# One wait per piece of weights instead of four in the down projection of a transformer block

## The reference

```python
x = x + attn(layernorm(x), wq, wk, wv, wo)
xn = layernorm(x)
g = einsum('th,ih->ti', xn, gate_w) * gate_s      # 2048 -> 5632
u = einsum('th,ih->ti', xn, up_w) * up_s
hdn = silu(g) * u
x = x + einsum('ti,hi->th', hdn, down_w) * down_s  # 5632 -> 2048
```

## Time and profile before

| | |
|---|---|
| median of 3 runs | 3502.85 us |
| the profiled execution, its own time | 3511.11 us |
| its slowest core (core 3), first to last instruction | 3509.5 us |
| spans of the 8 cores | 3486.0 to 3509.5 us |
| PE matmul busy on core 3 | 2981.4 us (85%), 13472 matmuls |
| VectorE, ScalarE busy | 930.2 us (27%), 896.3 us (26%) |
| mean granted TensorE clock, cores | 0.909 to 0.922 of 2.4 GHz |
| down projection, first span | about 1893 to 2348 us |
| down projection, second span | about 3030 to 3489 us |

### The profile page before, as it was taken

One profiled execution on the slowest core, in us unless ns is written; L12 is line 12 of the kernel. 1 busy time (PEld: TensorE's weight loads), 2 busy tenths in 40 slices (PEclk: granted clock), 3 DMA queues, 4 the chain that ended last, 5 costly groups with the idle time before them and its releaser, 6 DMA issues.

```text
span 3509.5 us, 43939 instructions; the slowest of 8 cores (3486.0 to 3509.5 us)
## 1 busy us (share of the span) xinstructions
PE 2981.4 (85%) x13472; PEld 1390.3 (40%) x13472; DVE 930.2 (27%) x1998; ACT 896.3 (26%) x1744; POOL 83.1 (2%) x158
## 2 busy tenths in 40 slices
PE   4999977777779969999998787677999999868766
PEld 2454444444434444444443232224444444323222
DVE  4532178888823121111110102112111111010111
ACT  2420056666622032222221121103222222101000
POOL 0000000000000000000000000000000000000000
PEclk9999976777689969999999899896999999989888
DMA  6212210000062234444444334323444444333432
GB/s 157 97 35 39 37 34 6 8 8 8 3 136 87 91 87 117 108 120 114 108 122 96 86 106 114 84 58 99 109 113 121 109 116 119 98 85 100 113 85 59
DMA packets 69058, 297.67 MB, mean 85 GB/s; under 512 B 7780, under 2 KB 14052, under 8 KB 49380
## 3 DMA queue, kind: packets, MB, share of 16 engines
q1 hardware_dynamic: 44360, 204.67, 17.7%
q0 software_dynamic: 24480, 90.19, 15.1%
HBM read 364.03 MB, written 20.97 MB: 110 GB/s over the span
## 4 chain that ended last, share of the span: by engine, by line
PE 78%; issue 8%; DVE 6%; DMA 6%; ACT 2%; DVEq 0%; ACTq 0%; SPq 0%; POOLq 0%
PE pb L849 18%; PE pb L745 17%; PE pb L751 17%; PE pb L445 6%; PE pb L682 6%; PE pb L518 4%; DMA out<-osb 3%; DVE pb L487 2%; PE pb L404 2%; PE pb L653 2%; PE pb L473 1%; PE pb L386 1%; ACT xnst L643 1%; PE pb L522 1%; DMA wot<-wot 1%
## 5 line engine op out<-in xcount | busy, mean ns | idle before, releaser
L745 PE MATMUL pb<-xn2T,gub 128*128 128x512 bf16 x2816 | 639.1, 380 | 0.0
L751 PE MATMUL pb<-xn2T,gub 128*128 128x512 bf16 x2816 | 636.5, 379 | 0.0
L849 PE MATMUL pb<-dnb,h_a 128*128 128x512 bf16 x2240 | 543.4, 386 | 101.4 <-PE pb L849 88.1
L745 PEld LDWEIGHTS pb<-xn2T,gub 128*128 128x128 bf16 x2816 | 276.0, 98 | 334.1 <-issue 3.9
L751 PEld LDWEIGHTS pb<-xn2T,gub 128*128 128x128 bf16 x2816 | 275.6, 98 | 332.2
L849 PEld LDWEIGHTS pb<-dnb,h_a 128*128 128x128 bf16 x2240 | 201.9, 98 | 443.0 <-issue 251.0
L756 ACT ACTIVATE silub<-pb,gs_sb 128x512 f32<-128x512 f32 x176 | 121.2, 689 | 929.2 <-PE pb L745 929.2
L770 DVE SCALAR_TENSOR_TENSOR h_a<-pb,us_sb,silub 128x512 bf16<-128x512 f32 x144 | 108.1, 751 | 889.1 <-PE pb L751 889.1
L518 PE MATMUL pb<-idf,pr 128*128 128x128 f32 x768 | 201.6, 393 | 90.8 <-DVE stats L504 87.1
L809 ACT CAST dnb<-dnf 128x2048 bf16<-128x2048 f32 x44 | 83.6, 1899 | 764.2 <-PE pb L849 672.1
L682 PE MATMUL pb<-wot,aoall 128*128 128x512 bf16 x1024 | 228.8, 387 | 18.9 <-DMA wot<-wot 18.9
(11 more groups left out here) (77 smaller groups left out, 1919.2 us busy)
## 6 DMA issues: line engine op xcount, KB each, us to landing
gf<-gt SPq DMA_DIRECT2D x88, 1024.0 KB, 5.7
gub<-ut POOLq DMA_DIRECT2D x88, 512.0 KB, 7.2
dnf<-dnt SPq DMA_DIRECT2D x44, 1024.0 KB, 4.9
dnb<-dnt POOLq DMA_DIRECT2D x44, 512.0 KB, 5.2
xb<-xo SPq DMA_DIRECT2D x16, 1024.0 KB, 4.8
xb<-xo SPq DMA_DIRECT2D x32, 512.0 KB, 5.0
out<-osb SPq DMA_DIRECT2D x64, 256.0 KB, 2.8
wqb<-wqt POOLq DMA_DIRECT2D x16, 512.0 KB, 5.2
```

Source lines behind the costliest of these rows:

```text
L745: e.matmul(ph(gb), lhsT=gub[gsl][:, dc, :], rhs=xn2T[:, dc, 512 * grp:512 * grp + 512], start=(dc == 0), stop=(dc == DC - 1))
L751: e.matmul(ph(ub), lhsT=gub[usl][:, dc, :], rhs=xn2T[:, dc, 512 * grp:512 * grp + 512], start=(dc == 0), stop=(dc == DC - 1))
L849: e.matmul(ph(tt), lhsT=h_ap(i, tt), rhs=dnb[dsl][:, k, :], start=(i == 0), stop=(i == IC - 1))
```

## The change

The four operations of a piece become one. For `i4` > 0, one operation of 32 matmuls replaces four of 8. For `i4` = 0, the eight single matmuls stay, and one operation of 24 (k = 1 to 3) replaces three of 8. The matmuls, their operands and their order are the same. The first operation of 24 or 32 names what the replaced ones named together: the inner blocks `r_h`, the piece's weights, the eight banks.

```diff
-            for k in range(4):
-                i = 4 * i4 + k
-                if i == 0:
-                    for tt in range(8):
-                        em("tensor", ... e.matmul(ph(tt), lhsT=h_ap(0, tt), ...
-                    continue
-                em("tensor", lambda e, i=i, k=k, dsl=dsl: [
-                    e.matmul(ph(tt), lhsT=h_ap(i, tt),
+            if i4 == 0:
+                for tt in range(8):
+                    em("tensor", ... e.matmul(ph(tt), lhsT=h_ap(0, tt), ...
+                em("tensor", lambda e, dsl=dsl: [
+                    e.matmul(ph(tt), lhsT=h_ap(k, tt),
                              rhs=dnb[dsl][:, k, :],
-                             start=(i == 0), stop=(i == IC - 1))
-                    for tt in range(8)],
-                   reads=[r_h[i], r_dnb[dsl]],
-                   writes=[r_pb[tt] for tt in range(8)], n=8)
+                             start=False, stop=False)
+                    for k in range(1, 4) for tt in range(8)],
+                   reads=[r_h[1], r_h[2], r_h[3], r_dnb[dsl]],
+                   writes=[r_pb[tt] for tt in range(8)], n=24)
+            else:
+                em("tensor", lambda e, i4=i4, dsl=dsl: [
+                    e.matmul(ph(tt), lhsT=h_ap(4 * i4 + k, tt),
+                             rhs=dnb[dsl][:, k, :],
+                             start=False, stop=(4 * i4 + k == IC - 1))
+                    for k in range(4) for tt in range(8)],
+                   reads=[r_h[4 * i4 + k] for k in range(4)] + [r_dnb[dsl]],
+                   writes=[r_pb[tt] for tt in range(8)], n=32)
```

More of the change, by code:

```diff
@@ L836, in build_nc @@
                 ln2_stats(1, (ci - 4) // 4)
-            for k in range(4):
-                i = 4 * i4 + k
-                if i == 0:
-                    for tt in range(8):
[L841 to L846, removed]
-                    continue
-                em("tensor", lambda e, i=i, k=k, dsl=dsl: [
-                    e.matmul(ph(tt), lhsT=h_ap(i, tt),
-                             rhs=dnb[dsl][:, k, :],
-                             start=(i == 0), stop=(i == IC - 1))
-                    for tt in range(8)],
-                   reads=[r_h[i], r_dnb[dsl]],
-                   writes=[r_pb[tt] for tt in range(8)], n=8)
+            if i4 == 0:
+                for tt in range(8):
+                    em("tensor", lambda e, tt=tt, dsl=dsl:
+                       e.matmul(ph(tt), lhsT=h_ap(0, tt),
+                                rhs=dnb[dsl][:, 0, :],
+                                start=True, stop=False),
+                       reads=[r_h[0], r_dnb[dsl]],
+                       writes=[r_pb[tt]])
+                em("tensor", lambda e, dsl=dsl: [
+                    e.matmul(ph(tt), lhsT=h_ap(k, tt),
+                             rhs=dnb[dsl][:, k, :],
+                             start=False, stop=False)
[10 more added lines that the diff above has]
+                   writes=[r_pb[tt] for tt in range(8)], n=32)
             if ci + 2 < NCH:
```

## The result

The changed kernel takes 3385.07 us in the median of 10 runs (3379.55 to 3723.24). The ratio to the kernel before is 0.965, with a 95% interval of 0.9637 to 0.9662: 3.5% faster. The forecast was 3378 us and 124.5 us off 3502.85, a ratio of 0.9645. The five runs that are left of before have a median of 3507.2 us, the seven of after 3384.16, which is 123.0 us apart. The profiled execution of after took 3381.15 us, 130.0 less than that of before, and is read on its slowest core, core 6.

A forecast was written before the change was run, and what follows sets the result against it. The prediction took TensorE, waiting for its own last matmul in the down projection, as the bound: 256 x 0.494 = 126.5 us, less 2.0 absorbed, gives 124.5 off 3502.85, or 3378.4 us, range 3364 to 3400.

The forecast's parts named there:

- 256 waits of PE for the matmul just issued: Down projection groups: merging removes 256 of 344 waits of PE for its own last matmul, 0.494 us each, 126.5 us.
- the median becomes 3502.85 - 124.5: Whole kernel: the saving of 124.5 us taken from the median before, 3502.85, giving 3378.4 us.
- the clock: After each eviction: the lower clock comes back as fast as before; one more cold matmul per eviction would be 1.7 us.
- the part hidden at the stage starts: Start of both down stages: removed waits of the first piece return as waiting for the second piece's cast, 2.0 us lost.
- the eviction: Six evictions where PE waits for VectorE and output stores: order unchanged, no net change, 15 us allowed both ways.
- the transposes' pauses: Layer-norm transposes: read as waits for their own groups of 4 matmuls, 0.26 us each, as evidence against growth with bumps.
- rival (b): Down projection waits: only the idle part comes back, 84.7 us less a little at the starts; 3419.5 us, chance 0.02.
- Weights in time: Down stages' weight transfers and casts: still early enough at 7.40 us per piece, with 4 us slack at the latest cast.
- Rival (a): Down projection: weights come late and PE waits at the piece's head; 37 us, giving 3415 us, chance 0.04.
- Rival (d): Both down stages: denser matmuls are granted less clock, making the kernel slower, up to 192 us, 3570; chance 0.02.
- (e): Merged down groups still pause inside, perhaps from fetching instructions, so nothing is gained; 3503 us, chance 0.02.
- (c): Remaining waits at down group heads grow with the run's length as semaphore bumps queue; 3463 us, chance 0.02.

## Where the prediction was right and where it was not, point by point

The mechanism held: 256 waits of PE for the matmul just issued, at 0.494 us each. What failed is smaller. The step that put the time too low is "the median becomes 3502.85 - 124.5": its starting time was 4.3 us low. Three terms of the sum were mis-sized and nearly cancel: the clock, put at nothing, cost 2.1 us; the part hidden at the stage starts, put at 2.0, was 2.9; the eviction, put at nothing, gave back 2.6 in the mean of the eight cores. In the reasoning, two readings of rows failed: the pauses were taken as one price with scatter, and the transposes' pauses were taken for waits of the same kind. Each is told below.

*The size and place of the gain.* Right. The two down stages, from the first L842 or L840 to the end of the last matmul, took 456.4 and 459.5 us before and take 392.2 and 395.9 after: 127.8 us less, all of the difference of the spans (3509.5 - 3379.5 = 130.0) but 2. These are core 3 of one execution and core 6 of the other; in the mean of the eight cores the stages went from 908.6 to 782.7 us, 125.9 less, and the rest of the kernel from 2588.2 to 2587.6. The forecast was 124.5.

*256 waits at 0.494.* Right, both factors. The idle time of L849 without the cast's wait went from 112.9 to 27.0 us, 85.9 (84.7 forecast as the idle part), and the overlap of 256 last matmuls, 256 x 0.163, is 41.7 us, together 127.6 where 126.5 stood. That the tail counts as well, not just the idle time that the profile prints, was the choice that mattered: rival (b), at 3419.5, would have been 35 us off. Groups of 16, groups of 4 and no own waits at all give 0.47 to 0.52 us a wait in the down stages (85.7 / 166, 157.8 / 336, 166.9 / 336), so the price holds within 5% at three other numbers of waits. One slip of counting changes nothing: a d-block has 11 pieces and a span 44, not a d-block 44; the sum uses 88 pieces, which is right.

*Absorbed at the stage starts.* Right in kind, 2.9 us instead of 2.0 (2.3 in the mean of the eight cores). The cause named for it (the first odd transfer behind the scales' load) was shown by moving that load. But the load that the prediction calls small is 1 MB and holds that transfer back by 5.1 to 6.4 us, and that four reloads lie right behind it was not seen.

*Weights in time.* Right. The cast after the third eviction is late against its DMA in the profile after too, and PE doesn't wait for it:

```profile
2210.93 1.90 ACT L809 CAST dnb<-dnf 128x2048 bf16<-128x2048 f32 x1 [29.27 <-DMA dnf<-dnt]
```

It ends at 2212.83, and its piece starts at 2218.00, 5 us later. Rival (a) falls. The statistics ended 1.05 us before the eviction was due (about 1 us forecast), by VectorE's timeline:

```profile
2181.10 0.16 DVE L632 RECIPROCAL stats<-stats 128x1 f32<-128x1 f32 x1 [26.50 <-ACT stats L630]
2182.32 0.69 DVE L868 TENSOR_TENSOR osb<-pb,dsb_sb 128x512 f32<-128x512 f32 x1 [1.05 <-PE pb L854]
```

*The eviction.* The order is as it was, and its waits are 93.8 us instead of 99.7, inside the 15 us left for it. Most of these 5.9 us is the choice of core: the cores read 86.5 to 99.7 before and 85.7 to 93.8 after, 2.6 less in the mean.

*The clock.* The granted clock of the down stages is 0.92 and 0.91 where it was 0.92 in both, and 1.00 between evictions. The first 24 or 32 matmuls behind a long pause lose 17.3 us in all to the lower level, where they lost 15.2. The term that the prediction put at nothing is thus 2.1 us over the eight long pauses; in the mean of the six cores whose traces have all matmuls it is 2.4. Why the clock comes back a little later is not shown. Rival (d), a lower granted clock over the whole stage, did not come: the cores read 0.910 to 0.921 over the kernel where they read 0.909 to 0.922, and with PE denser still (no own waits) the time fell as expected.

*The time itself.* 3378.4 is 6.7 us under the median of 3385.07. The step that failed here is the starting time: 3502.85 is the median of three runs, and the five that count in the end have 3507.2, which is 4.3 us. The change itself accounts for 1.5 (124.5 against 123.0), and 0.9 is the distance between the median of all ten runs and that of the seven.

The ledger: -85.9 idle, -41.7 tail, +2.9 cast, -5.9 eviction, +2.1 clock = -128.5, against -127.8 read from the stages.

*The two readings.* The prediction treated the 0.26 and the 0.36 as one scatter, and left "something in fetching instructions" as a possible cause of the longer pauses in (e). With the own wait last, every pause reads 0.15 us: both the step of 0.10 and the pauses of 0.40 to 0.54 are waits handled behind the own one. And its first argument against (c) does not hold. A layer-norm transpose group (L353) writes a bank that PE last wrote four transpose groups earlier, so its 12 pauses of 0.26 us are not waits for the group just ahead. Asking for a matmul two or three back leaves them as they are, 3.1 us in 12, in the kernels that take 74 and 144 us out of the down stages. What causes them stays open; without own waits they shrink to 0.15. Rival (c) was still wrong, but it is the groups of 4 and 16 and the single bump that show it.

## What to carry over

A helper that makes an engine wait for its own last instruction hides a pause in every group, and the profile shows it as an engine that waits for itself. Count the waits and take start to start, not the idle column: here 0.494 us each, of which the idle column shows 0.331. Once such a wait asks for a matmul that started more than 0.71 us ago it is free, so dropping it, reaching further back or merging groups are three ways to the same gain, and dropping it brings most (a ratio of 0.951 against 0.965). If a wait has to block, put it last in its list.

## What the runs showed of the hardware

- With one or two more waits behind it, PE's wait for its own matmul of 128x512 is free once that matmul started 0.71 us ago: 0.494 us is lost at one back, 0.274 at two, 0.05 at three, none at five. With the own wait last in order, 0.308 is lost at one back.
- A satisfied wait mostly costs 0.10 us behind the blocking one (pauses of 0.26 and 0.36 us, 0.15 with none behind) and nothing ahead of it. The longer pauses, of up to 0.54 us, went away with it.
- 32 semaphore bumps in a run of matmuls 216 ns apart cost the same as one: 22.5 us in 72 waits with either.
- A stage can be short of a transfer at its start for a reason that is only order in a queue: the four reloads of 128 KB on one semaphore took 10.5 to 15.3 us, one after the other.
